# Eight-word register loads, waits once per four pairs, and landings counted in eights, in the two edge aggregations of a graph network kernel

## The reference, cut to what matters

```
# x: (12500, 256); src, dst: (200000,), edges sorted by dst; weight: (200000,)
msgs = layernorm(x)[src] * weight[:, None]           # layer 0: gather by src
agg  = segment_sum(msgs, dst, 12500)                  #          sum by dst
x    = x + agg @ W0.T + b0
x    = x + moe0(layernorm(x))
h    = layernorm(x) @ W1                              # layer 1: gather by dst
agg  = segment_sum(weight[:, None] * h[dst], src, 12500)   #     sum by src
x    = x + relu(batchnorm(agg + bias))
x    = x + moe1(layernorm(x), edge_index)             # gated by a graph attention
```

## Time and profile before

| | |
|---|---|
| Median of 3 runs | 8193.99 us (8183.62 to 8203.72) |
| Profiled execution, span from first to last instruction | 8556.1 us (the page gives no time around it) |
| Mean granted clock of TensorE over the span | 0.784 of full speed |
| First aggregation, from the first gather to the last | 211 to 2485.6 us, last add at about 2526 us |
| Second aggregation | 4122 to 6427.6 us, last add at about 6447 us |

### The profile page before, as it was taken

How to read it: one execution, slowest core, us unless ns; L and a number is a source line. 1 busy time by engine, 2 the same in 40 slices (tenths; PEclk the granted TensorE clock), 3 DMA queues, 4 the chain that set the end, 5 groups by cost and what they waited for, 6 DMA issues and landing times. The chain is left out here.

```text
span 8556.1 us, 91570 instructions
## 1 busy us (share of the span) xinstructions
PE 5764.1 (67%) x19687; PEld 3851.9 (45%) x19687; DVE 4500.6 (53%) x8804; ACT 3777.5 (44%) x9645; POOL 5818.2 (68%) x7545
## 2 busy tenths in 40 slices
PE   5454555555556999968465656565556888888866
PEld 4333333333335666644243434443333555555545
DVE  5354555545456999958454454554457222222227
ACT  5555555655554222226355555555555222222213
POOL 3666666666644222226688888888886688888875
PEclk8677767676665999989666767766678999999988
DMA  7333333333332111126333333333333322222218
GB/s 227 91 90 89 90 91 91 92 91 91 91 116 81 45 50 49 46 65 206 99 90 91 91 89 91 88 91 90 88 91 129 95 59 57 56 58 55 56 47 324
DMA packets 498681, 797.56 MB, mean 93 GB/s; under 512 B 121278, under 2 KB 363563, under 8 KB 498059
## 3 DMA queue, kind: packets, MB, share of 16 engines
q0 software_dynamic: 200256, 453.47, 19.5%
q1 hardware_dynamic: 297904, 338.22, 12.2%
HBM read 595.60 MB, written 197.30 MB: 93 GB/s over the span
## 5 line engine op out<-in xcount | busy, mean ns | idle before, releaser
L1013 PE MATMUL part<-rows,spread 128*128 x6656 | 2481.5, 527 | 1990.5 <-issue 984.0
L1013 PEld LDWEIGHTS part<-rows,spread 128*128 128x128 f32 x6656 | 1613.8, 261 | 2797.6 <-issue 2539.6
L970 DVE TENSOR_TENSOR agg<-agg,part 128x257 f32 (+1 forms) x3328 | 1405.1, 422 | 2230.5 <-PE part L1013 721.7
L953 POOL DMA_INDIRECT rows<-f,row x1563 | 1549.6, 991 | 733.8 <-issue 453.0
L1037 ACT ACTIVATE spread<-iota,place 128x128 f32<-128x128 f32 x3328 | 1016.1, 387 | 2038.2 <-PE part L1013 1309.5
L953 POOL DMA_INDIRECT rows<-h,row x1563 | 1550.5, 992 | 258.4 <-issue 256.3
L1952 POOL DMA_INDIRECT rows<-gat,src x1122 | 1077.9, 961 | 185.0 <-issue 185.0
L1043 ACT ACTIVATE spread<-spread,weight 128x128 f32<-128x128 f32 x3328 | 1017.5, 388 | 14.1 <-ACT spread L1039 0.3
L2030 PE MATMUL y_ps<-agg,hid 128*128 128x256 f32 x3136 | 765.4, 405 | 190.7 <-DVE y_all L2160 190.7
L2030 PEld LDWEIGHTS y_ps<-agg,hid 128*128 128x128 f32 x3136 | 640.9, 206 | 342.2 <-DVE y_all L2160 209.5
L404 POOL COPY spare<-pay 128x1024 f32<-128x1024 f32 x105 | 222.3, 2117 | 735.7 <-DVE pay L391 505.7
(11 more groups left out here) (400 smaller groups left out, 6449.2 us busy)
## 6 DMA issues: line engine op xcount, KB each, us to landing
expert_rows<-y_all SPq DMA_DIRECT2D x196, 256.0 KB
made<-expert_rows SPq DMA_DIRECT2D x49, 1024.0 KB
x<-x SPq DMA_DIRECT2D x42, 896.0 KB
rows<-f,row POOLq DMA_INDIRECT x1563
rows<-h,row POOLq DMA_INDIRECT x1563
rows<-gat,src POOLq DMA_INDIRECT x1122
xbuf<-zero SPq DMA_DIRECT2D x16, 1024.0 KB
x<-xbuf SPq DMA_DIRECT2D x32, 512.0 KB
```

Of the source, the lines that this page charges most:

```text
L953: pool.indirect_dma_start(out=rows[:, u, 0:D], out_offset=None, in_=table, in_offset=bass.IndirectOffsetOnAxis(ap=q.row[:, i:i + 1], axis= ...
L970: nc.vector.tensor_tensor(sum_t, sum_t, part[:, p % NB, 0:WIDE], ALU.add).then_inc(added, 1)
L1013: nc.tensor.matmul(part[:, p % NB, 0:WIDE], spread[:, p % (2 * BANKS), :], row_p, start=True, stop=True).then_inc(multiplied, 1)
```

## The change

Words from `q.tile` are loaded into registers eight at a time, on VectorE and TensorE, once per group of eight pairs. The plan's landing word counts groups of chunks and no longer chunks: (chunk + 8) shifted right by three, one more operation on VectorE. SyncE waits once per group of chunks, for 128 counts of one of four semaphores instead of 16 counts of each of eight, and counts `landed` by groups. The wait for `landed` moves from TensorE to ScalarE, which reads the word itself between its Relu and its Copies. TensorE waits once per four pairs for `spread_done` and `added`, each as far as the last of the four needs it; VectorE waits once per four pairs for `multiplied`, and as before for `added` before each add.

```diff
--- before.py
+++ after.py
@@ -105,8 +105,8 @@
 
 def load_tiles(nc, eng, q, first, regs):
 
-    for four in range(0, len(regs), 4):
-        eng.reg_load(regs[four:four + 4], q.tile[0:1, bass.ds(first + four, 4)])
+    for eight in range(0, len(regs), 8):
+        eng.reg_load(regs[eight:eight + 8], q.tile[0:1, bass.ds(first + eight, 8)])
     return [nc.s_assert_within(eng.snap(r), 0, BUCKETS - 1, skip_runtime_bounds_check_because="a tile counts buckets begun before a pair, of which the first is left out")
             for r in regs]
 
@@ -170,8 +170,8 @@
 
 def load_slots(nc, eng, q, first, regs):
 
-    for four in range(0, len(regs), 4):
-        eng.reg_load(regs[four:four + 4], q.tile[32:33, bass.ds(first + four, 4)])
+    for eight in range(0, len(regs), 8):
+        eng.reg_load(regs[eight:eight + 8], q.tile[32:33, bass.ds(first + eight, 8)])
     return [nc.s_assert_within(eng.snap(r), 0, RING * BANKS - 1, skip_runtime_bounds_check_because="a slot is a chunk's low bits")
             for r in regs]
 
@@ -223,7 +223,8 @@
     link(nc.vector.tensor_copy(w.tint[:, 0:m], w.tcol[:, 0:m]))
 
     link(nc.vector.tensor_scalar(w.tint[:, m:2 * m], plan.chunk[:, 0:m], RING * BANKS - 1, None, ALU.bitwise_and))
-    link(nc.vector.tensor_scalar(w.tint[:, 2 * m:3 * m], plan.chunk[:, 0:m], 1.0, None, ALU.add))
+    link(nc.vector.tensor_scalar(w.tint[:, 2 * m:3 * m], plan.chunk[:, 0:m], float(BANKS), None, ALU.add))
+    link(nc.vector.tensor_scalar(w.tint[:, 2 * m:3 * m], w.tint[:, 2 * m:3 * m], 3, None, ALU.arith_shift_right))
 
     link(nc.vector.tensor_scalar(w.gcol[:, :], k.qcol[:, 0:2], float(BANKS), float(BANKS), ALU.mult, ALU.add))
     for h in range(2):
@@ -910,7 +911,7 @@
         part = s.ps("part", [P, NB, 512])
         worded, rested = s.sem("worded"), s.sem("rested")
         sort_ps = [part[:, h, :] for h in range(2)]
-        gathered = [s.sem(f"gathered{u}") for u in range(SPAN)]
+        gathered = [s.sem(f"gathered{u}") for u in range(RING)]
         ready, squared, marked, spread_done, multiplied, added, landed, freed = (s.sem(n) for n in (
             "ready", "squared", "marked", "spread_done", "multiplied", "added", "landed", "freed"))
         with nc.Block() as block:
@@ -926,10 +927,9 @@
                     sp.sem_inc(freed, 1)
 
                 for j in range(CGROUPS):
-                    for i in range(j * BANKS, (j + 1) * BANKS):
-                        if i < FILLED:
-                            sp.wait_ge(gathered[i % SPAN], i // SPAN * 16 + 16)
-                        sp.sem_inc(landed, 1)
+                    full = min(BANKS, FILLED - j * BANKS)
+                    sp.wait_ge(gathered[j % RING], 16 * (j // RING * BANKS + full))
+                    sp.sem_inc(landed, 1)
                     if c is not None and j == 5:
                         tally_load(sp, c, gdst, 1)
                     if 2 <= j < CGROUPS - RING + 2:
@@ -951,22 +951,22 @@
                             pool.wait_ge(rested, i)
                         nc.gpsimd.memset(k.zero[:, 0:3 * P // 2], 0.0).then_inc(rested, 1)
                     pool.indirect_dma_start(out=rows[:, u, 0:D], out_offset=None, in_=table,
-                                            in_offset=bass.IndirectOffsetOnAxis(ap=q.row[:, i:i + 1], axis=0)).then_inc(gathered[u], 16)
+                                            in_offset=bass.IndirectOffsetOnAxis(ap=q.row[:, i:i + 1], axis=0)).then_inc(gathered[u // BANKS], 16)
 
             @block.vector
             def _(dve):
-                regs = [dve.alloc_register(f"tile{n}_{nc.next_id()}") for n in range(4)]
+                regs = [dve.alloc_register(f"tile{n}_{nc.next_id()}") for n in range(8)]
 
                 def add(g):
                     for u in range(BANKS):
                         p = g * BANKS + u
+                        if u == 0:
+                            tiles = load_tiles(nc, dve, q, p, regs)
                         if u % 4 == 0:
-                            tiles = load_tiles(nc, dve, q, p, regs)
-                        dve.wait_ge(multiplied, p + 1)
-
+                            dve.wait_ge(multiplied, p + 4)
                         if p:
                             dve.wait_ge(added, p)
-                        sum_t = agg[:, bass.ds(tiles[u % 4], 1), :].rearrange("p o d -> p (o d)")
+                        sum_t = agg[:, bass.ds(tiles[u], 1), :].rearrange("p o d -> p (o d)")
                         nc.vector.tensor_tensor(sum_t, sum_t, part[:, p % NB, 0:WIDE], ALU.add).then_inc(added, 1)
 
                 if begun:
@@ -1004,11 +1004,10 @@
                 for p in range(EPAIRS):
                     if p % BANKS == 0:
                         at = load_slots(nc, pe, q, p, slots)
-                        upto = pe.value_load(q.tile[64:65, p // BANKS:p // BANKS + 1], min_val=1, max_val=ECH)
-                        pe.wait_ge(landed, upto)
-                    pe.wait_ge(spread_done, p + 1)
-                    if p >= NB:
-                        pe.wait_ge(added, p - NB + 1)
+                    if p % 4 == 0:
+                        pe.wait_ge(spread_done, p + 4)
+                        if p + 3 >= NB:
+                            pe.wait_ge(added, p + 4 - NB)
                     row_p = rows[:, bass.ds(at[p % BANKS], 1), :].rearrange("p o d -> p (o d)")
                     nc.tensor.matmul(part[:, p % NB, 0:WIDE], spread[:, p % (2 * BANKS), :], row_p, start=True, stop=True).then_inc(multiplied, 1)
                     if p % BANKS == BANKS - 1:
@@ -1038,6 +1037,8 @@
                     act.wait_ge(squared, (g + 1) * BANKS)
                     nc.scalar.activation(spread[:, h, :], spread[:, h, :], ACT.Relu, scale=-1.0, bias=k.ones[:, 0:1]).then_inc(marked, 1)
                     act.wait_ge(marked, g + 1)
+                    upto = act.value_load(q.tile[64:65, g:g + 1], min_val=1, max_val=CGROUPS)
+                    act.wait_ge(landed, upto)
                     for u in range(BANKS):
                         p = g * BANKS + u
                         nc.scalar.activation(spread[:, p % (2 * BANKS), :], spread[:, p % (2 * BANKS), :], ACT.Copy, scale=q.weight[:, p:p + 1]).then_inc(spread_done, 1)
```

## The result

The change makes the kernel slower: 8249.06 us (median of four runs, 8246.19 to 8253.66) against 8197.9 us for the kernel before, run beside it on the same chip. The ratio is 1.0064, 95% interval 1.005 to 1.0078: 51 us lost, where 129 were forecast to be won. The profiled execution of after agrees with its runs; the one of before that the forecast rests on does not agree with its own, at 8556 us, and this turned out to be the point.

What follows compares the result with a forecast made beforehand. POOL was taken to set the pace, with 243 and about 70 us of late consumer on top. First aggregation -125 - 30 + 60 - 15 = -110, second -20, sum -130: 8194 - 130 = 8064, say 8065; range 7870 to 8280.

Steps and rivals of the forecast that it cites:

- POOL sets the pace: Both aggregations: POOL's gathers set the pace; gathering and tails together take 4640 of 8556 us.
- 243 and about 70 us in which the consumer is late: POOL's waits for freed groups in first and second aggregation, which a faster ACT, PE and DVE could return.
- The signs that I had asked for: First aggregation: POOL's wait falls from 271 to 120 to 180 us, DVE's "issue" from 510 to under 400.
- the first rival: Aggregations: POOL alone is left, all its waits for the consumer go, 7866 us; chance 0.17.
- Control instructions, -125: First aggregation's slow stretches: 10 instead of 16 control instructions per four pairs on PE and DVE, 125 us saved.
- Loads, and the -30 for fast stretches: First aggregation: PE saves about 0.9 us per group change, ACT loses 0.6 per group; net -30 us.
- Fours, +60: First aggregation, after 66 sort swaps: PE restarts after four adds instead of one, 60 us lost, bounds 0 and 125.
- Tail, -15: After the first aggregation's last gather: the 40.4 us tail shortens with the consumer's lag, by 15 us.
- Second aggregation, -20: Second aggregation: shorter loads against later landing counts, with only 70 us of waiting to return; -20, between -65 and +127.
- The second: Rival, no change: slow stretches belong to the profiled execution, only tail and loads move, 8185 us; chance 0.17.
- The third: Rival, PSUM between PE and DVE: hand-over in fours costs more than control instructions give, 8314 us; chance 0.19.
- The sign that was to refute every case: ACT's wait for landing lasting over 300 us while POOL stands still would make every case wrong.

Runs made afterwards that it cites:

- before_again: The unchanged kernel before, profiled once more: span 8192.1 us; 8193.8 beside 8187.6 us.
- nomem_before: Kernel before without the memset that POOL runs ahead of each gather of the second aggregation: 8000.23 us, ratio 0.9769 to before.
- load8: Kernel before with only the eight-word loads of tiles and slots on PE and DVE: ratio 1.0011 to before.
- act_landed: Kernel before with only the landing word and its wait moved from PE to ScalarE, still counting chunks: ratio 1.0021 to before.
- fours: Kernel before with only the waits once per four pairs on PE and DVE: ratio 1.0011 to before.
- nomem_after: Changed kernel without the memset ahead of each gather of the second aggregation: 8024.64 us, ratio 0.9798 to before.
- hold_first: Changed kernel with ScalarE's payload copy for the sort issued ahead of its wait for landed: ratio 1.0049 to before.
- chunks_hold: Changed kernel with landings counted in chunks again and ScalarE's payload copy ahead of its wait: ratio 1.0022 to before.
- sp_groups: Kernel before with only SyncE counting landings in groups of eight chunks, PE still waiting for them: ratio 1.0041 to before.
- after_chunks: Changed kernel with landings counted one chunk at a time again: ratio 1.0040 to before.

## Why the prediction was wrong, point by point

**What bounds the kernel.** "POOL sets the pace" held. "On top of it come 243 and about 70 us in which the consumer is late" was the failing step: of the kernel as it runs these are 0. The -125 and the -20 of the sum were shares of a loss that the timed runs never had. The number that spoke against it stood in the text: the span was 362 us above the median, and all of POOL's waits for SyncE (271 + 71 = 342 us) fit into that. I carried the microseconds over unscaled, when they had to be struck out. The signs that I had asked for would even have confirmed a gain, the first rival's: POOL's wait is gone and DVE's "issue" fell to 34.2 us; but in before_again the one is gone as well, and the other is not among the releasers of DVE's adds.

The Trainium skill ("Perfetto Trace Analysis", What "DMA-bound" means) calls a kernel bound by the issuing sequencer where that track is solid. By the disturbed trace POOL's was not; in before_again it is, in the first aggregation with no gap but its own 0.30 us, and the 187 us of nomem_before agree with the rule.

**Control instructions, -125.** Measured 0: at 0.05 us in place of 0.70 there was nothing to save. That they became fewer (the page counts 82598 instructions, 91570 before) gained nothing either.

**Loads, and the -30 for fast stretches.** Sized rightly, worth nothing: behind POOL a shorter group of the consumer doesn't show, so the -30 was 0 too (load8 alone is at 1.0011, act_landed at 1.0021, both on the slower side). An eight-word load takes 0.59 us on PE and 0.60 on DVE, against the 0.6 taken; ScalarE's word takes 0.277 + 0.147 + 0.018 = 0.44 us, between the bounds 0.4 and 0.8. Sequencers of PE, DVE and ACT in after:

```profile
L174 PEldq TENSOR_LOAD <-tile x416: 587/591/1459, 194.7 to 6125.7; - x139
...
L109 DVEq TENSOR_LOAD <-tile x416: 593/597/845, 194.5 to 6130.3; - x139
...
L1040 ACTq TENSOR_LOAD <-tile x416: 272/277/481, 198.1 to 6123.6; - x139
L1040 ACTq FUSED_REGOPS  x416: 147/147/162, 198.6 to 6123.9; - x139
L1040 ACTq SEQ_ASSERT  x416: 18/18/18, 198.8 to 6124.1; - x139
```

**Fours, +60.** The sign was right, the place wrong. POOL's pace covers the hand-over inside the first aggregation (2038.3 us against 2038.9); what shows of fours alone is 3.4 and 5.7 us in the tails, and 10 us in the runs. Its second aggregation is 9.7 us longer, but so is load8's by 9.4, in both mostly by longer gathers, and of before there is one undisturbed trace: what this comes from is not shown. The Trainium skill ("Perfetto Trace Analysis", Optimizing Scalar/DVE Operations) says that where Scalar or Vector are not saturated but leave others idle, breaking up their instructions may let work finish sooner; fours, which makes the waits coarser, at 1.0011 [1.0002, 1.002], agrees in sign.

**Tail, -15.** It became longer instead, by 13.9 and 16.2 us, half of the loss. The consumer follows POOL at its heels: PE's wait for landing, 36.8 and 14.7 us in the earlier trace rows, is 1739.6 us in before_again, and the same idle time is ScalarE's in after. The waits of before_again, whole run:

```profile
PE part L1013 <- SPq L932: 1739.6, 382, 20.7
```

and of after:

```profile
ACT spread L1044 <- SPq L932: 1681.3, 363, 9.7
```

A chunk that is passed on with its seven fellows is therefore not covered by a full ring, as I had put it: the ring is nearly empty, and the consumer works that much later all along. It costs nothing until POOL stops. Then it is all there: DVE in the tail of before_again (last gather over at 2234.3) has begun its last swap already, and 16 adds remain; in after (last gather over at 2249.9) the swap and 24 adds do. DVE's timeline of before_again:

```profile
2232.29 1.23 DVE L386 TENSOR_TENSOR key<-key 128x1024 f32<-128x1024 f32 x1
2233.55 2.44 DVE L390 COPY_PREDICATED pay<-mask,pay 128x1024 f32<-128x1024 uint16 x1
2236.02 2.44 DVE L391 COPY_PREDICATED pay<-mask,spare 128x1024 f32<-128x1024 uint16 x1
...
2249.07 0.42 DVE L970 TENSOR_TENSOR agg<-agg,part 128x257 f32 x1 [0.21 <-DVE agg L970]
```

and of after:

```profile
2253.33 2.12 DVE L970 TENSOR_TENSOR agg<-agg,part 128x257 f32 x4 [3.51 <-PE part L1012]
2256.15 2.12 DVE L970 TENSOR_TENSOR agg<-agg,part 128x257 f32 x4 [0.70 <-PE part L1012]
2258.19 1.22 DVE L385 TENSOR_TENSOR mask<-key 128x1024 uint16<-128x1024 f32 x1
...
2264.43 2.43 DVE L392 COPY_PREDICATED pay<-mask,spare 128x1024 f32<-128x1024 uint16 x1
2267.95 2.12 DVE L970 TENSOR_TENSOR agg<-agg,part 128x257 f32 x4 [1.08 <-issue]
...
2276.85 2.12 DVE L970 TENSOR_TENSOR agg<-agg,part 128x257 f32 x4 [0.49 <-PE part L1012]
```

By the single parts, the count in groups gives 9.6 and 11.0 us of this, fours 3.4 and 5.7, ScalarE's wait 2.2 and 2.3; in after itself, taking the count in groups back returns 8.8 and 8.1.

**What the sum did not have at all: the gathers' length.** Of the first aggregation's 15.9 us, 15.5 are in the gathers themselves (1563.1 to 1578.6; nomem_after, whose first aggregation is the same code, has 1572.3, so one trace tells this to about 6 us). The prediction named the payload copy behind ScalarE's new wait as something that DVE's swap waits for, and gave it no price. The wait is small in after, larger in act_landed and gone in hold_first; the gathers take 1578.6, 1576.3 and 1557.6 us, so their length doesn't go with the length of the wait. The swap's first predicated copy, in the first aggregation, of before_again:

```profile
L390 DVE COPY_PREDICATED pay<-mask,pay 128x1024 f32<-128x1024 uint16 x66 | 108.9, 1650 | 2.3
```

of after:

```profile
L391 DVE COPY_PREDICATED pay<-mask,pay 128x1024 f32<-128x1024 uint16 x66 | 109.4, 1657 | 20.0 <-ACT spare L1048 18.6
```

of act_landed:

```profile
L390 DVE COPY_PREDICATED pay<-mask,pay 128x1024 f32<-128x1024 uint16 x66 | 109.9, 1665 | 132.0 <-ACT spare L1047 132.0
```

of hold_first:

```profile
L391 DVE COPY_PREDICATED pay<-mask,pay 128x1024 f32<-128x1024 uint16 x66 | 109.3, 1656 | 2.3
```

These copies take 2.4 us in 21 of the 66 swaps and 1.3 us in 45. Gathers that start beside the long ones last two to three times as long. The last swap but one of after, first DVE:

```profile
2239.33 2.46 DVE L391 COPY_PREDICATED pay<-mask,pay 128x1024 f32<-128x1024 uint16 x1 [0.85 <-ACT spare L1048]
2241.82 2.45 DVE L392 COPY_PREDICATED pay<-mask,spare 128x1024 f32<-128x1024 uint16 x1
```

and POOL beside it:

```profile
2238.40 0.95 POOL L953 DMA_INDIRECT rows<-f,row  x1 [0.30 <-issue]
2239.65 2.76 POOL L953 DMA_INDIRECT rows<-f,row  x1 [0.30 <-issue]
2242.72 2.18 POOL L953 DMA_INDIRECT rows<-f,row  x1 [0.30 <-issue]
```

In before_again the last swap but one stretches two gathers too, but by less; DVE, then POOL:

```profile
2209.19 2.43 DVE L390 COPY_PREDICATED pay<-mask,pay 128x1024 f32<-128x1024 uint16 x1
2211.66 2.44 DVE L391 COPY_PREDICATED pay<-mask,spare 128x1024 f32<-128x1024 uint16 x1
...
2210.28 1.97 POOL L953 DMA_INDIRECT rows<-f,row  x1 [0.30 <-issue]
2212.55 2.17 POOL L953 DMA_INDIRECT rows<-f,row  x1 [0.30 <-issue]
```

That a copy held back by ScalarE's wait lengthens the gathers is shown by hold_first and chunks_hold, which return 21.0 and 20.3 us of them. The rows show how: in both traces the first stretched gather ends 0.62 to 0.63 us after the first copy, but in after it starts 0.32 us into the copy and in before_again 1.09 us, so it lasts 0.8 us longer. In before_again, hold_first and chunks_hold no first copy waits, and in each of the 65 swaps beside the gathers a gather starts 1.08 to 1.20 us into it; then it takes at most 2.01 us beside a long copy and is hardly stretched beside a short one (at most 1.03). In after 28 first copies wait, the gather starts anywhere from 0.03 us on, and it takes up to 3.01 us beside a long copy and 1.92 beside a short one. Summed over the 65 swaps these gathers take 97.9 us in after and 83.4 in before_again, 14.5 of the 15.5 us. The length of a wait does not matter for this, only where in POOL's 1.25 us the copy then starts. In act_landed all 65 wait and these gathers take 107.8 us; its gathers grow by 13.2 us in all, since those beside the swap's comparison are stretched less (by 12.5 us in all, 26.9 in before_again).

Other operations of DVE stretch gathers too: at 2205.56 in before_again a gather beside the swap's comparison takes 1.89 us. The shorter gathers of nomem_after lie in its second aggregation, where no predicated copy runs: what they take above 0.95 us beside the sort's min and max and the count's 128x1536 operation is 87 us in nomem_before and 69 in nomem_after. Why the change shortens these is not shown.

The Trainium skill ("SBUF — State Buffer", SBUF: two separate sides) describes VectorE and GpSimd sharing one pair of ports as an exclusive lock, so that GpSimd can't write a DMA's descriptors while certain VectorE operations hold it. The stretched gathers agree with that; whether these copies take the lock, no run here shows.

**Second aggregation, -20.** It became 15.5 us longer. Gathers take 6.7 us and memsets 1.2 more, together 7.9, no more than in load8 and fours (8.9 and 9.6), so these are not told from the difference between traces. The other 7.4 us are idle time before the gathers, which also stands in sp_groups and hold_first and not in after_chunks and chunks_hold: it comes with the count in groups. It lies in 15 gaps, most of them 0.82 us in place of 0.17, a multiple of 96 gathers apart; what POOL does in them the traces don't show, and it stays open.

The sum of the traces: 13.9 + 16.2 (tails) + 15.9 + 15.5 (gathering) = 61.5, and -1.7 elsewhere; the spans differ by 59.8, the runs by 51.

**The rivals.** The second had the right cause (slow stretches that belong to the profiled execution), and its sign came, a shorter trace and no faster runs; its price was wrong: 8185, as if the tail could then only shorten. Its chance of 0.17 was far too low for what stood in favour of it. The first fell, since its 243 + 60 us didn't exist. The third had the right sign, for a mechanism that doesn't bind: PE waits more for DVE's adds in after (293.8 us in the second aggregation, 18.5 in before_again), but behind POOL. The sign that was to refute every case, ScalarE over 300 us in its landing wait while POOL stands still, came by half: 1681 us of it, and POOL never stood still.

## What to carry to other kernels

Before a loss in a trace is priced, compare the trace's span with the untraced times; if they differ by more than runs differ, find a loss of that size, and give it no value until a second profile shows it. Where one engine issues without a gap, as POOL here, work taken from the others was worth nothing, and what made them hand over later was paid when the issuing engine ended. The time was in the issuing engine's own work: without the memset the kernel takes 8000.23 us, 0.9769 [0.9756, 0.9782], better than either version.

## What was not expected of the hardware

A gather that POOL issues in 0.95 us takes 1.86 to 3.01 us when it starts during a 2.4 us predicated copy of DVE (in after, from 0.07 us into the copy on): it ends 0.62 to 0.65 us after the copy, whenever it began. So the moment at which another engine does its work, which POOL does not wait for, moved the bound by 1% of a stage (1556.7 to 1578.6 us of gathers in 2055). And one profiled execution had stretches in which each control instruction took 0.70 us instead of 0.05, 364 us in all by its span, which none of the eleven other traces showed.
